# Moving the product of U and delta from VectorE to GpSimd in the second stage of a hybrid block

## The reference

```python
u = silu(conv(x) + conv_b)                      # 1024 channels
dt_lr, Bm, Cm = split(einsum('bld,rd->blr', u, x_proj_w))
delta = softplus(einsum('blr,dr->bld', dt_lr, dt_proj_w) + dt_proj_b)
def step(h, xs):                                # 16 states n for each channel
    dA = exp(d_t[..., None] * A)
    h = h * dA + (d_t * u_t)[..., None] * B_t[:, None, :]
    y_t = einsum('bdn,bn->bd', h, C_t)
y = ys + u * D_param
```

## Time and profile before

| | us |
|---|---|
| median of 3 runs | 3651.24 (3647.86 to 3652.23) |
| the profiled execution | 3647.6 |
| its span, first to last instruction | 3645.8 |

### The profile page before, as it was taken

The page is one execution under the profiler, slowest core; times in us unless marked ns, Lnnn a source line. Parts: engine busy times, 40 slices in busy tenths (PEclk is TensorE's granted clock), DMA queues, the critical chain, the costliest instruction groups (busy, mean ns, idle before and its releaser), DMA issues.

```text
span 3645.8 us, 46163 instructions
## 1 busy us (share of the span) xinstructions
PE 3261.5 (89%) x12672; PEld 2351.4 (64%) x12672; DVE 3274.3 (90%) x6015; ACT 2449.1 (67%) x4758; POOL 2452.8 (67%) x1943
## 2 busy tenths in 40 slices
PE   4888994989999999999999999999999999975738
PEld 4666662667667676767676767667676766653515
DVE  5899983199999999999999999999999999999991
ACT  4777772177777777777776768676777767765640
POOL 0344343078878696969696969796969697857570
PEclk9999997999999999999999999999999999987868
DMA  2122222211111211111111111111112120111010
GB/s 104 64 81 73 82 64 73 78 27 44 30 47 33 52 30 47 33 44 37 42 39 39 41 38 39 39 40 38 41 39 47 31 54 24 53 25 34 24 35 6
DMA packets 119376, 165.35 MB, mean 45 GB/s; under 512 B 8544, under 2 KB 84192, under 8 KB 118624
## 3 DMA queue, kind: packets, MB, share of 16 engines
q1 hardware_dynamic: 119136, 162.63, 16.1%
HBM read 128.39 MB, written 25.69 MB: 42 GB/s over the span
## 4 chain that ended last, share of the span: by engine, by line
POOL 29%; DVE 24%; issue 16%; PE 9%; ACT 3%; DVEq 1%; DMA 0%; POOLq 0%; SPq 0%; ACTq 0%
POOL dBu L865 17%; DVE D L1312 11%; POOL yacc L878 11%; PE W L1065 6%; DVE prod L1331 3%; DVE D L1334 2%; DVE U L1258 1%; DVE dBu L1292 1%; DVE U L1304 1%; PE D L1143 1%; PE D L1147 1%; PE W L1097 1%; ACT L915 1%; DVE delta L1299 1%; DVE yacc L1343 1%
## 5 line engine op out<-in xcount | busy, mean ns | idle before, releaser
L1312 DVE TENSOR_TENSOR_SCAN D<-D,hc,dBu 128x256 f32<-128x256 f32 x2048 | 1445.4, 748 | 0.0
L865 POOL TENSOR_TENSOR dBu<-U,BC 128x512 f32<-128x512 f32 x1024 | 1293.8, 1274 | 180.9 <-DMA BC<-bc_scratch 144.7
L1065 PE MATMUL W<-nT,wffn 128*128 128x256 f32 x5632 | 1234.0, 382 | 15.4 <-ACT nT L904 15.4
L1008 ACT ACTIVATE D<-delta,A 128x256 f32<-128x256 f32 x2048 | 892.8, 468 | 519.6 <-DVE yacc L1343 490.2
L1065 PEld LDWEIGHTS W<-nT,wffn 128*128 128x128 f32 x5632 | 1062.8, 189 | 193.0 <-ACT nT L904 21.4
L878 POOL TENSOR_TENSOR yacc<-yacc,prod 128x512 f32<-128x512 f32 x736 | 935.0, 1270 | 247.3 <-DVE prod L1331 245.3
L1097 PE MATMUL W<-wffn,hT 128*128 128x512 f32 (+1 forms) x1408 | 617.4, 594 | 12.1 <-DVE hT L1227 11.9
L1065 PE MATMUL W<-nT,win 128*128 128x256 f32 x2048 | 472.0, 392 | 91.8 <-ACT U L935 75.2
L1065 PEld LDWEIGHTS W<-nT,win 128*128 128x128 f32 x2048 | 400.0, 197 | 167.6 <-ACT U L935 81.2
L1331 DVE TENSOR_TENSOR prod<-D,BC 128x512 f32<-128x512 f32 x736 | 501.4, 681 | 0.0
L1097 PEld LDWEIGHTS W<-wffn,hT 128*128 128x128 f32 (+1 forms) x1408 | 262.7, 190 | 331.9 <-issue 307.8
(11 more groups left out here) (117 smaller groups left out, 3140.2 us busy)
## 6 DMA issues: line engine op xcount, KB each, us to landing
BC<-bc_scratch SPq DMA_DIRECT2D x256, 256.0 KB, 4.6
XM<-x_scratch SPq DMA_DIRECT2D x29, 512.0 KB, 4.7
X<-x_scratch SPq DMA_DIRECT2D x17, 512.0 KB, 3.6
ix<-idx SPq DMA_DIRECT2D x33, 255.0 KB, 2.9
X<-x SPq DMA_DIRECT2D x16, 512.0 KB, 3.3
XR<-x SPq DMA_DIRECT2D x16, 512.0 KB, 3.4
x_scratch<-XR SPq DMA_DIRECT2D x16, 512.0 KB, 3.7
out<-X SPq DMA_DIRECT2D x16, 512.0 KB, 2.8
```

Of the source, the lines that this page charges most:

```text
L865: nc.gpsimd.tensor_tensor(dBu[e % 4][:], U[:, 2 * j:2 * j + 2, :], BC[slot][:, 0:1, :].to_broadcast([P, 2, CH]), ALU.mult).then_inc(s_dBu, 1)
L1008: N_.activation(D[:, m, :], delta[:, m, :], ACT.Exp, scale=A[:, m, n:n + 1]).then_inc(s_dA, 1)
L1065: last = T_.matmul(dst, lhsT, rhs, start=(n == 0), stop=(n == len(terms) - 1))
L1312: V.tensor_tensor_scan(D[:, m, :], D[:, m, :], dBu[e % 4][:, m % 2, :], hc[:, n, m:m + 1], ALU.mult, ALU.add).then_inc(s_scan, 1)
```

## The change

The four products of U and delta leave VectorE's program. They go into GpSimd's, each ahead of the outer product of the same pair, with the waits that they had. The semaphore `m_du` is now counted up by GpSimd, and GpSimd itself waits for it.

```diff
+                    def times_u(j):
+
+                        pair = slice(2 * j, 2 * j + 2)
+                        pool.wait_ge(m_skip, ME * i + 2 * (j + 1))
+                        pool.wait_ge(m_bc, i + 1)
+                        pool.wait_ge(m_delta, 4 * i + j + 1)
+                        nc.gpsimd.tensor_tensor(U[:, pair, :], U[:, pair, :], delta[:, pair, :], ALU.mult).then_inc(m_du, 1)
+
                     for e in range(4):
+                        times_u(e)
                         outer(e)
...
                     for j in range(ME // 2):
-                        pair = slice(2 * j, 2 * j + 2)
                         dve.wait_ge(m_ln, 4 * i + j + 1)
                         for h in range(2):
                             m = 2 * j + h
                             step_ = V.scalar_tensor_tensor(delta[:, m, :], D[:, m, :], bdt[:, m:m + 1], dBu[j][:, h, :], ALU.add, ALU.max)
                         step_.then_inc(m_delta, 1)
-                        dve.wait_ge(m_skip, ME * i + 2 * (j + 1))
-                        dve.wait_ge(m_bc, i + 1)
-                        dve.wait_ge(m_delta, 4 * i + j + 1)
-                        V.tensor_tensor(U[:, pair, :], U[:, pair, :], delta[:, pair, :], ALU.mult).then_inc(m_du, 1)
```

## The result

The changed kernel takes 3677.6 us (median of 4 runs, 3670.1 to 3680.6) against 3649.6 us before: ratio 1.0076, 95% interval 1.0061 to 1.0091. It is **slower by 28 us**, where 3640.9 and a range up to 3652 were forecast. The profiled executions, 3678.8 us of span against 3645.8, differ by 33 us.

What follows compares the result with a forecast made beforehand. VectorE was taken to set the chunk's length. Twelve ordinary heads at 0.93, minus two late-load heads at 0.95, plus two last chunks at 1.3, minus 16 × 0.1 for veps gave 10.3 us: 3640.9 us, range 3632 to 3652.

Steps and rivals of the forecast that it cites:

- the rival of deltas holding off GpSimd: At each head, deltas block GpSimd's first product until 3.4 instead of 0.95: 25 us slower, 3676; chance 0.05.
- The last two chunks: GpSimd has only two adds in four there and keeps up, so each head gains 1.3 us.
- Loads of B and C: Late-loads rival: loads land too late to hide the first product; 14 us slower, 3665; chance 0.06.
- the 0.85 at step 7: At a typical head, loop step 7 ends at 21.83 instead of 22.68 us after the first delta: gain 0.85.
- e=4 starts at 11.34 + 1.30 + 0.59: In the ramp, fourth outer product, two scans, product with C: step 4 starts at 13.23 instead of 14.48, 1.25 gained.
- late by 1.6 us: GpSimd runs some 1.6 us late at step 7, but just catches up by step 8's product.
- the term of 0.1 us for veps: VectorE's small statistics operation behind step 8 grows from 0.78 to about 0.8 to 0.9; 0.1 us charged per chunk.
- The row for the upper end, 1.86 us: Longest veps duration in the profile; taken as the bad end of the veps charge, a loss of 1.1 us.
- the forecast's first rival: No measurable gain: slightly longer GpSimd instructions, a longer-held veps or the feed-forward take the 0.85; 3648 to 3651; chance 0.27.
- TensorE has some 3 us to spare per chunk: At the chunk's end TensorE waits about 3 us for conv taps, so VectorE's gain up to that passes through.
- Theory C: Follow-up theory, not in the prediction: what was lost is TensorE's granted clock at the chunk changes.

Runs made afterwards that it cites:

- both edits: Changed kernel (products on GpSimd) with a third prod buffer and veps on GpSimd: 3621.2 us, ratio 0.9921.
- the kernel before with the same edits: Kernel before (products on VectorE) with a third prod buffer and veps on GpSimd: 3631.8 us, ratio 0.9956.

## Why the prediction was wrong

**Right.** The product on GpSimd lasts 1.26 to 1.28 us (1.27 forecast), a pair takes 2.58 (2.58), the first one starts 1.04 after the first delta (0.95). The deltas beside it last 472 to 486 ns, so the rival of deltas holding off GpSimd is out. The last two chunks gained 1.07 and 1.32 by step 7 (1.3). Loads of B and C weren't the cause: GpSimd waited 1.5 us for them in the whole changed kernel. And the 0.85 at step 7 appeared as 0.75 once everything else was out of the way: 22.05 with both edits, against 22.80 in the kernel before with the same edits.

**Wrong, first step: "e=4 starts at 11.34 + 1.30 + 0.59".** The product with C was taken as free to follow the scans. It has a wait of its own, on GpSimd's add two products earlier, and GpSimd's first add now ends at 1651.85, 13.92 after the first delta. The forecast itself had GpSimd late by 1.6 us and asked only who waits for its outer products, not who waits for its adds. Measured: 1.05 + 0.28 us per chunk. Without them (third buffer) step 7 ends at 22.06, a gain of 0.62, as the ramp runs 0.23 behind the forecast; with them it ends at 23.21, a loss of 0.53 (0.31 of wait at step 7 falls away). This step isn't enough for the 28 us, nor does it add to them: without the buffer's wait the changed kernel took 3677.4. It costs where veps is gone: 3635 against 3621.

**Wrong, second step, and the one that made the loss: the term of 0.1 us for veps.** It was worked out with veps let in at the next instruction boundary of GpSimd. It is let in when GpSimd's list pauses: of 116 veps of over 0.3 us, in the four traces that have such, every one ends within 0.04 us of the end of a GpSimd instruction behind which GpSimd paused. The forecast's own times, a start at 26.5 and a list through at 29.75, would have given 3.2 us by that rule, and with the third buffer it lasted 3.20. Step 9 then starts at 29.8 with or without the buffer's wait, 1.76 later than before. The row for the upper end, 1.86 us, is longer than one GpSimd instruction and said so; it was read as a chance mishap. Measured: 1.25 us more in an ordinary chunk (0.95 in the two with a late load, 1.28 in the first, 3.14 against 1.86). And this term isn't independent of the others: with the third buffer VectorE came 1.15 us earlier and veps grew by 1.17. A late GpSimd was named in the forecast's first rival ("a veps held for half an instruction more"), but priced as the end of a gain, not as a loss. The measured time lies beside the 3676 of the rival in which deltas hold off GpSimd; that is chance, since GpSimd's first product started at 1.04.

**Wrong, third: TensorE has some 3 us to spare per chunk.** The pause at the chunk change isn't slack: it stayed at 2.8 to 3.0 us in kernels whose period ran from 178.3 down to 174.1. By the program, TensorE's last matmuls of a chunk begin after an evacuation of ScalarE that follows VectorE's loop (TensorE waits 0.41 us for it at 1762.38 in the kernel before), so the pause moves along. Its slack lay in such waits: 9.7 us inside the feed-forwards and 4.8 before those last matmuls, 1.2 per chunk from 920 to 3100 us in the kernel before, and 0.3 in all with the first product and veps on GpSimd. The floor of the first feed-forward is the add at 78.47. None of this touched the result here, where the period grew.

**Not in the forecast at all:** 7.4 of the 33 us, at the chunk changes. The gate's 32 matmuls take 7.17, 8.86 or 10.1 us; in the kernel before 8.86 in eight changes of fourteen and 7.17 in six, in the changed kernel 10.0 to 10.2 in four and 7.17 in three. In the longer ones the granted clock is 0.50, its lower level of 1.2 GHz, and comes back within the gate. The pause ahead of them is 2.96 us in both kernels, so the change doesn't lengthen it. The kernel before with veps on GpSimd has 7.2 us more at these changes too, and the changed kernel with veps on GpSimd 2.2, so they don't go with the products' move; what sets in which changes the clock falls stays open. Theory C is a part of the loss, then, not its cause.

## What to carry to other kernels

When work is moved to an engine that runs a fixed list, count everything it hands out, not only what the moved work feeds: here a buffer of two entries tied VectorE to GpSimd's adds, and being late by 1.6 us cost 14 us (3635 against 3621), more than the products' move gained. Don't average a tiny operation whose duration varies tenfold: find what it ends with in the trace, and if it ends when the other engine pauses, every edit that keeps that engine busy lengthens it. Such operations of two elements per partition were worth 19 us for one of them and 65 for both in the kernel before, as much as the 62 us of busy time that the change moved.

## What the runs showed of the hardware

- VectorE's tensor_scalar of two elements from SBUF to SBUF waits over the boundary between two GpSimd instructions that follow each other without a pause (2.03 and 3.20 us, in the first chunk 4.32), and lasts 0.17 when GpSimd is idle. The same work in two operations of one element isn't held off at all (0.21 us for both).
- nmr, of the same size but a scalar_tensor_tensor with two SBUF inputs, mostly ends at the first such boundary (0.95 to 1.22 us). Once in 310 it went over two and lasted 3.23. What decides this stays open.
- VectorE's U x delta (128x512, two SBUF inputs) is let in at the boundary: with only the first product on GpSimd it ended 0.55 us after GpSimd's outer product, and the outer product that followed without a pause took 1.71 us instead of 1.27.
- After a pause of 2.96 us TensorE's granted clock was at its lower level at the start of the gate in most chunk changes (8 of 14 in the kernel before, 11 of 14 in the changed one). After pauses of 1.69 to 1.95 us, in thirteen changes of each of four kernels, it never was; after the 1.97 us of their last change it was in two of the four.
